# Two attention and mixture-of-experts blocks on one core: expert results scattered to token order by GpSimd inside the expert phases, in place of gathers behind them

## What is computed

```python
x = x + xattn0(layernorm(x), ctx)          # 16 heads of 16
x = x + ffn0(layernorm(x))                 # layer 0
x = x + xattn1(layernorm(x), ctx, mask)
x = x + ffn1(layernorm(x))                 # layer 1
# ffn: shared MLP + routed experts, E = 16 experts of 256 -> 128 -> 256
#   layer 0: the 4 best experts of a token (from the 2 best of 4 groups), sigmoid weights, times 2.5
#   layer 1: the 2 best experts of a token, softmax weights
#   y[token] = sum over its k experts of w * (silu(x Wg) * (x Wu)) Wd
```

## Time and profile before

| what | value |
|---|---|
| median of 3 runs | 2484.33 us (2482.01 to 2484.53) |
| the profiled execution: its own time | 2487.88 us |
| its span, first to last instruction | 2486.0 us |
| busy share PE / DVE / ACT / POOL | 82% / 59% / 43% / 45% |
| moved by DMA | 292.77 MB, mean 118 GB/s |

### The profile page before, as it was taken

One profiled execution on the slowest core, in us unless ns is written; L12 is line 12 of the kernel. 1 busy time (PEld: TensorE's weight loads), 2 busy tenths in 40 slices (PEclk: granted clock), 3 DMA queues, 4 the chain that ended last, 5 costly groups with the idle time before them and its releaser, 6 DMA issues.

```text
span 2486.0 us, 52846 instructions
## 1 busy us (share of the span) xinstructions
PE 2044.5 (82%) x16352; PEld 1599.3 (64%) x16353; DVE 1467.8 (59%) x4591; ACT 1068.5 (43%) x2276; POOL 1121.9 (45%) x1595
## 2 busy tenths in 40 slices
PE   4999999999965999999948989889998849997000
PEld 3777777777754878777736766666666637786000
DVE  3677777777762444444436877777777624443333
ACT  2555555555522333333325555555555513332000
POOL 1455555555556000000056777777777341001676
PEclk8999999999987999999969999999999969999555
DMA  5222222222226444444434333333333154444555
GB/s 204 58 79 80 79 80 80 82 82 78 76 83 148 150 146 150 151 146 151 149 123 171 102 101 101 103 101 107 98 102 101 41 105 150 150 149 132 177 175 169
DMA packets 206442, 292.77 MB, mean 118 GB/s; under 512 B 34230, under 2 KB 155320, under 8 KB 205880
## 3 DMA queue, kind: packets, MB, share of 16 engines
q1 hardware_dynamic: 164199, 185.12, 22.9%
q0 software_dynamic: 37584, 102.81, 13.2%
q10 hardware_dynamic: 4608, 4.20, 1.3%
HBM read 155.69 MB, written 136.33 MB: 117 GB/s over the span
## 4 chain that ended last, share of the span: by engine, by line
PE 59%; POOL 18%; issue 12%; DVE 4%; DMA 4%; ACT 2%; SPq 1%; POOLq 1%; DVEq 0%; ACTq 0%
PE ps L1435 16%; POOL ygath L615 10%; PE ps L1443 7%; PE ps L1371 5%; POOL xsort L559 4%; PE ps L1448 4%; PE ps L1309 3%; PE ps L1287 3%; PE ps L1321 3%; PE ps L1263 3%; PE ps L1346 2%; PE ps L1380 2%; PE ps L1454 2%; POOL rstd L631 2%; PE ps L1230 2%
## 5 line engine op out<-in xcount | busy, mean ns | idle before, releaser
L1435 PE MATMUL ps<-wgu,ygath 128*128 x1664 | 441.3, 388 | 27.6 <-issue 23.0
L559 POOL DMA_INDIRECT xsort<-xn,xidx x384 | 386.7, 1007 | 134.7 <-issue 133.4
L615 POOL DMA_INDIRECT ygath<-ysort,yidx x384 | 372.5, 970 | 152.1 <-issue 99.1
L928 DVE TENSOR_REDUCE mx<-ps 128x16 f32<-128x1920 f32 x128 | 276.2, 2158 | 191.1 <-PE ps L1287 190.8
L1175 DVE TENSOR_TENSOR ygath<-ygath,ps 128x128 f32<-128x128 f32 x416 | 119.7, 288 | 442.8 <-ACT ygath L842 442.8
L1435 PEld LDWEIGHTS ps<-wgu,ygath 128*128 128x128 f32 x1664 | 285.3, 191 | 73.8 <-issue 51.6
L607 POOL CAST yidx<-rows_of 128x8 uint32 (+1 forms) x64 | 12.9, 201 | 682.2 <-SPq L297 680.4
L1371 PE MATMUL ps<-W,wsgu 128*128 128x256 f32 x1024 | 253.3, 391 | 13.7 <-ACT rt L789 12.9
L846 ACT ACTIVATE ygath<-ps 128x256 f32<-128x256 f32 x416 | 159.8, 384 | 231.4 <-PE ps L1448 231.2
L1443 PE MATMUL ps<-wd,ygath 128*128 x832 | 248.1, 380 | 2.8 <-DVE ygath L1187 2.8
L842 ACT ACTIVATE ygath<-ps 128x128 f32<-128x128 f32 x416 | 115.5, 278 | 301.4 <-PE ps L1435 301.3
(11 more groups left out here) (174 smaller groups left out, 3836.2 us busy)
## 6 DMA issues: line engine op xcount, KB each, us to landing
ygath<-xsort SPq DMA_DIRECT2D x416, 128.0 KB, 2.1
ysort<-ygath SPq DMA_DIRECT2D x208, 256.0 KB, 2.3
based<-XO SPq DMA_DIRECT2D x64, 256.0 KB, 2.3
XB<-in_x SPq DMA_DIRECT2D x32, 256.0 KB
wgu<-in_wgu SPq DMA_DIRECT2D x2, 4096.0 KB, 13.7
XB<-based SPq DMA_DIRECT2D x32, 256.0 KB
X<-based SPq DMA_DIRECT2D x32, 256.0 KB
out_x<-X SPq DMA_DIRECT2D x32, 256.0 KB, 2.3
```

The lines of the kernel that those rows point to most:

```text
L559: e.indirect_dma_start(out=xsort, in_=xn2[s][:, t, :], in_offset=None, out_offset=bass.IndirectOffsetOnAxis(ap=xidx[s][:, t * 4 + k:t * 4 ...
L615: e.indirect_dma_start(out=ygath[s][:, t * 4 + k, :], out_offset=None, in_=ysort, in_offset=bass.IndirectOffsetOnAxis(ap=yidx[s][:, t * 4 ...
L928: e.tensor_reduce(mx[:, r].rearrange("p j t h -> p j (t h)"), ps[:, 4 * s:4 * s + 4, 0:4 * LK].rearrange("p j (x k) -> p j x k", k=LK), AX ...
L1435: mm = e.matmul(ps[:, 2 + h, 0:2 * F], xtT[h][:, c, :], wgu[:, bass.ds(x * (DC * 2 * F) + c * 2 * F, 2 * F)], start=(c == 0), stop=(c == D ...
```

## The change

- A row of `xsort` gets 16 more floats (`ROW` = 272): for each expert, the place (token times k, plus which k) at which the result is to stand in token order. DVE writes them in a new step, `aim_rows`, behind `weigh_experts`: a product of 128 x 128 floats (64 in layer 1) and a sum. The zero rows that fill up a region carry places behind the last token.
- In the expert stage DVE takes the column of the tile's expert out of the loaded rows into `yidx` (one 128 x 1 copy a tile, between `yt` and `hT`), for which it reads four expert numbers into registers each fourth tile. POOL writes each result tile to `yrows` with one indirect DMA. SP's stores are gone, and SP waits for the index copy (`eI`) before it loads over a tile. DVE waits for the scatter (`yst`) of the tile four before when it writes `yt`, where it waited for a store.
- `all_rows`, `find_rows` and all gathers are gone. In attention 1 SP loads the 8 rows of a token with one plain DMA (1 MB a sequence); `pack_weights1` now comes behind POOL's scatters.
- The last pass is unrolled with four buffer sets: SP issues both loads (256 and 512 KB a sequence), DVE adds, ACT issues the store.
- Attention 1's order on POOL, ACT and DVE is changed (`ORDER`); its PE string is the same cycle, begun at another step.
- The write of spare rows at the start is two DMAs, issued once the constants have come.

```diff
-    "Pool1": "rstd1:a xb:b gather:m rstd2:c scatter:d",
+    "Pool1": "xb:a rstd2:b scatter:c rstd1:m",
...
-        xsort = nc.dram_tensor("xsort", [XROWS, D], F32).ap()
-        ysort = nc.dram_tensor("ysort", [NT[0] * P, D], F32).ap()
+        xsort = nc.dram_tensor("xsort", [XROWS, ROW], F32).ap()
+        yrows = nc.dram_tensor("yrows", [YROWS, D], F32).ap()
...
+        def routed(L):
+
+            return yrows[0:NTOK * TOPK[L], :].rearrange("(b t p k) d -> b p t (k d)", b=B, t=QT, k=TOPK[L])
...
                 if L == 1:
+                    e.dma_start(ygath[s][:].rearrange("p (t k) d -> p t (k d)", t=QT),
+                                routed(0)[bass.ds(b, 1)].rearrange("o p t x -> (o p) t x")).then_inc(sig["ld", s], 16)
...
                     for r in range(4):
 
+                        e.wait_ge(eI[r % 2], c2[2 + r // 2])
                         e.wait_ge(eT_ps[r % 2], c2[2 + r // 2])
                         apart(e)
                         load(r, row[r])
-                        if r % 2 == 1 and regs:
-                            store(n - 5 + r, r // 2, c2[r // 2])
...
+            for b in range(B):
+                r = b % 4
+                if b >= 4:
+                    e.wait_ge(fin_st[r], 16 * (b // 4))
+                e.dma_start(Xf[r][:], based[b]).then_inc(fin_ld[r], 16)
+                e.dma_start(Yf[r].rearrange("p (t k) d -> p t (k d)", t=QT), routed(1)[b]).then_inc(fin_ld[r], 16)
...
+            def expert_phase(L):
+
+                t0 = NT[0] // 4 * L
+
+                def step(n, r, w, c2):
+                    if isinstance(n, int) and n < 4:
+                        return
+                    q, h, c = tile(4, r, w, c2)
+                    e.wait_ge(eY[h], c)
+                    apart(e)
+                    i = q + 4 * (1 - r // 4)
+                    e.indirect_dma_start(
+                        out=yrows, in_=yt[q], in_offset=None,
+                        out_offset=bass.IndirectOffsetOnAxis(ap=yidx[:, i:i + 1], axis=0),
+                    ).then_inc(yst[q], 16)
...
-                all_rows()
+                expert_phase(L)
                 if L == 0:
                     pack_weights1()
...
+            for b in range(B):
+                e.wait_ge(fin, b + 1)
+                e.dma_start(out[b], Xf[b % 4][:]).then_inc(fin_st[b % 4], 16)
...
+            def aim_rows(L, u, s):
...
+                apart(e)
+                link(e.tensor_tensor(at_e, oh, bc(dest, 3, E), ALU.mult), "c_rt", s, L, u)
+                e.tensor_reduce(xn2[s][:, :, D:ROW], at_e.rearrange("p t k e -> p t e k"), AX.X, ALU.add)
...
-                        if q % 2 == 0 and not (edge and n < 8 and L == 0):
-                            e.wait_ge(yst[q // 2], (w - 1) * 16)
+                        if not (edge and n < 8 and L == 0):
+                            e.wait_ge(yst[q], (w - 1) * 16)
                         e.tensor_copy(yt[q], ps[:, 6 + h, 0:D]).then_inc(eY[h], 1)
+                    if not (edge and n >= NT[L]):
+                        if r % 4 == 0:
+                            e.load(expert_regs, exp_tab[0:1, bass.ds(n * 2 + 12, 4)])
+                            experts[0] = [e.snap(x, min_val=0, max_val=E - 1) for x in expert_regs]
+                        e.wait_ge(xl[r % 4], 16 * w + 16)
+                        apart(e)
+                        e.tensor_copy(yidx[:, r:r + 1], xt[r % 4][:, bass.ds(experts[0][r % 4] + D, 1)]
+                                      ).then_inc(eI[r % 2], 1)
                     if not (edge and (n < 3 or n > NT[L] + 2)):
                         _, h, c = tile(3, r, w, c2)
                         e.wait_ge(eHT_ps[h], c)
                         e.tensor_copy(hT[h], ps[:, 4 + h, 0:P]).then_inc(eHT[h], 1)
```

More of the change, by code:

```diff
@@ L213, in build @@
         xn = [sb(f"xn{s}", [P, QT, D]) for s in range(2)]
-        xn2 = [sb(f"xn2{s}", [P, QT, D]) for s in range(2)]
+        xn2 = [sb(f"xn2{s}", [P, QT, ROW]) for s in range(2)]
         xnT = [sb(f"xnT{s}", [P, DC, LQ]) for s in range(2)]
@@ L232, in build @@
         ygath = [sb(f"ygath{s}", [P, QT * 4, D]) for s in range(2)]
[L233 to L235 removed]
+        yidx = sb("yidx", [P, 8], U32)
         xidx = [sb(f"xidx{s}", [P, QT * 4], U32) for s in range(2)]
@@ L275, in build @@
         xl = [sem(f"xl{r}") for r in range(4)]
-        yst = [sem(f"yst{r}") for r in range(2)]
+        yst = [sem(f"yst{r}") for r in range(4)]
+        eI = [sem(f"eI{r}") for r in range(2)]
         eT_ps, eT, eGU, eG, eH, eHT_ps, eHT, eD, eY = (
@@ L341, in run_steps, with four @@
             t0, last = NT[0] // 4 * L, NT[L] // 4
-            def four(w, regs, steps, ahead=False):
+            def four(w, regs, steps, par=0, ahead=False):
                 n4 = (w - t0) * 4
@@ L503, in expert_phase @@
                     four(e.snap(w), True)
[L504 to L507, removed]
             e.wait_ge(zero_ok, 1)
-            e.dma_start(xsort[E * REG:XROWS, :].rearrange("(n p) d -> p n d", p=P), bc(zero[:], 1, E)
-                        ).then_inc(zfill, 16)
+            spare = xsort[E * REG:XROWS, :].rearrange("(n p) d -> p n d", p=P)
+            e.dma_start(spare[:, :, 0:ROW - 1], bc(zero[:, 0:ROW - 1], 1, E)).then_inc(zfill, 16)
+            with nc.allow_non_contiguous_dma(reason="one number a spare row, once"):
+                e.dma_start(spare[:, :, ROW - 1:ROW], cc(C_DUMP + E, E).unsqueeze(2)).then_inc(zfill, 16)
             e.wait_ge(init, 6)
@@ L527, in _ @@
             end_phase(e, 4)
[L529 to L539, removed]
-                                ).then_inc(sig["st", s], 16)
-            for s in range(2):
-                e.wait_ge(sig["st", s], ended("st", s) + NIT * 16)
+            for b in range(B):
[4 more added lines that the diff above has]
+                e.dma_start(Yf[r].rearrange("p (t k) d -> p t (k d)", t=QT), routed(1)[b]).then_inc(fin_ld[r], 16)
         @block.gpsimd
         def _(e):
-            e.memset(zero[:], 0.0).then_inc(zero_ok, 1)
+            e.memset(zero[:], 0.0)
             for s in range(2):
@@ L671, in attention_phase @@
                     e.wait_ge(sig["sc", s], at("sc", L, NIT - 1))
+            def expert_phase(L):
[11 more added lines that the diff above has]
+                    ).then_inc(yst[q], 16)
+                run_steps(e, L, step, 2)
+                for q in range(4):
+                    e.wait_ge(yst[q], 16 * (t0 + NT[L] // 4))
             for L in range(2):
@@ L682, in _ @@
                 end_phase(e, 2 * L + 2)
-            for s in range(2):
-                find_rows(s, 0, NIT)
-                gather(1, s, range(QT))
-            with e.Fori(1, NIT) as u:
-                for s in range(2):
-                    e.wait_ge(fin[s], u)
-                    find_rows(s, u, NIT + u)
-                    gather(1, s, range(QT))
         @block.scalar
@@ L856, in _ @@
                 end_phase(e, 2 * L + 2)
+            for b in range(B):
+                e.wait_ge(fin, b + 1)
+                e.dma_start(out[b], Xf[b % 4][:]).then_inc(fin_st[b % 4], 16)
+            for r in range(4):
+                e.wait_ge(fin_st[r], 16 * (B // 4))
         @block.vector
```

162 lines of the change are left out of this document (69 added, 93 removed), and 2 rows, old and new, of the table PER.

## The result

The changed kernel takes **2448.55 us** (median of 4 runs, 2444.13 to 2449.02) against 2484.4 us before (4 runs beside it, 2482.01 to 2484.53). The ratio is 0.9854, its 95% interval 0.9837 to 0.9871. It is faster, by 36 us in place of the 83 forecast, and 2448.55 lies inside the range, near its upper end. The profiled execution has a span of 2447.0 us, 39.0 less than the 2486.0 of before.

What follows compares the result with a forecast made beforehand. Bounds: POOL's gathers in attention 1 and the last pass, a PE-DVE ring without slack in the expert stages, PE in attention 0. Sum -90 - 46 - 5 + 2 + 3 + 53 + 0.5 = -83, so 2401 us; range 2345 to 2452.

Steps and rivals of the forecast that it cites:

- the register load's term: Expert stages, each fourth tile: DVE's register load between `yt` and the index copy adds 0.35 us, bounds 0.05 and 0.6.
- +53: Both expert stages: four index copies and two register loads, 1.02 us a round of 8 tiles, 52 rounds; +16 to +94.
- The ring without slack: Expert stages: PE and DVE wait on each other, 3.26 us for two tiles; anything between `yt` and `hT` lengthens it.
- 19.97 us a half: Attention 1: without gathers PE and DVE set this pace in place of 21.79, for -46 us (-60 to -33).
- little at the end: Attention 1: an unspecified small gain added to 24 halves times 1.82 us, making -46.
- the 345 taken: Last pass: transfer rate in GB/s, 97 us for 33.5 MB; 105 us in place of 195, so -90.
- Landing and packing: Stage ends: scatters landing after both expert stages cost +3 us, POOL packing weights behind its scatters +2.
- The wait that was to go for -5: Start of attention 1: ACT's normalising waits for POOL's 8 gathers of the second sequence; without them -5 us.
- Scatters as the pace of the expert stages: Rival, expert stages: at 2.3 us a scatter +229 in place of +53, 2577 us; chance 0.07 including similar-sized causes.
- Hidden index work: Rival, expert stages: DVE's sequencer runs ahead and one column costs nothing; +5 in place of +53, 2353 us; chance 0.17.
- DVE as the bound of attention 1: Rival, attention 1: 21 us a half in place of 19.97 loses 25 us of the gain, 2426 us; chance 0.13.
- A buffer's cycle as the bound of the last pass: Rival, last pass: buffer cycle, not rate, sets it, 14 us for 4 sequences, 120 us, 2416; no separate chance.

## Why the prediction was wrong in its size

The sign came out, and in each stage what was said to bind it. What failed is the size of the terms, and every stage came out longer than forecast. The sum missed by 44 us of span: 25 in the expert stages, 9 in attention 1, 3 to 4 in the last pass, 5 at the stage ends, 1 or 2 in attention 0. The largest miss is the register load's term: 0.35 us put on a loading tile, 0.69 measured. That 2448.55 lies inside the range is owed to wide bounds: that of the expert stages reached +94.

- **The expert stages, +78 for +53: the step that failed is the register load's.** The forecast had 0.5 us for the load, 0.2 for the register work on both sides, less 0.34 hidden behind `yt`: 0.35, twice in eight tiles. The load itself was about right, 0.60 in one loading tile and 0.34 in the other (0.47 on average), and the 0.34 was hidden. The register work was not 0.2 but some 0.55: the rows of 0.09, 0.19 and 0.06 and the pauses between them (1.17 us from `yt` at 900.06 to the index copy, less 0.60). About half of what stands behind the load belongs to the index copy, its wait for the row and its address, which the forecast counted into the 0.08 of that copy. So the delays were 0.83 and 0.54, 1.37 in eight tiles in place of 0.70, and their mean of 0.69 is over the term's own upper bound of 0.6. The index copy was 0.06, costed at 0.08. 4 * 0.06 + 1.37 = 1.6 us for eight tiles, 1.53 measured, times 52 = +80. The ring without slack is borne out by the load at the head of the step and by experts 1 without a load: nine tenths of the loss go when the load goes from there. The Trainium skill, "DMA: Bandwidth & Descriptors", Latency and other measured facts, has 600 ns as a floor for such a load; DVE's median here is 352 ns and its least 341, so the row decides; some 600 appear in fewer than half of the loads, mostly in each second one.
- **Attention 1, -37.5 for -46.** The forecast's 19.97 us a half was right for the plain loads: with the orders of before a half takes 616.75 / 31 = 19.90, and the stage gains 44.3. The diff also changed the orders, and I costed that at nothing; the half became 20.11 (623.5 / 31), which takes 6.7 back. That is this stage's failed step. The "little at the end" in the -46, 2.3 us, had no row either: the last three halves before the change already took 19.8 each. `aim_rows` is covered, as forecast.
- **The last pass, -86.5 for -90.** 321 to 324 GB/s at a share of 0.95 to 0.97 in place of the 345 taken. The bound was the right one, and so was the cycle of some 10 us: 10.2 with two sets, 10.9 with three. The step that was mis-sized is the rate.
- **Stage ends, +4.9 for 0.** Landing and packing were costed (+1.5 each, +2) and are there: the packing 1.8, the last scatter's landing 2.5 from its start. POOL's drain behind its scatters was not: 4.3 us behind experts 0, 2.8 behind experts 1. Before, POOL's drains of these stages began at 807.6 and 2060.4 us, long before the ends. So SP's first load of attention 1 comes 10.3 us behind the last `yt`, 2.9 before: 7.4 more for the 3.5 costed. The wait that was to go for -5 went: from SP's first load to ACT's first normalised rows it is 14.6 us in place of 23.3. From there to the first `rsum` it is 3.1 longer, and why stays open.
- **Attention 0, +1.7 for +0.5.** In the kernels with the change the stretch from the first `rsum` to the first `hm` is 725.7 to 732.4 us, before 724.7 in the one profile there is. A small loss is likely; what makes it stays open.
- **The rivals.** Scatters as the pace of the expert stages: POOL waits 338 us for `yt`, DVE never for a scatter. The Trainium skill's rule ("SBUF — State Buffer", Who interferes with whom), by which copies of DVE in its fast modes block GpSimd, no run here shows: the 416 scatters took 0.95 to 1.02 us each beside DVE's copies out of PSUM. Hidden index work became true only when it was put where it hides. DVE as the bound of attention 1: at 17.2 of 20 us beside PE's 19.15 it was not. A buffer's cycle as the bound of the last pass: true with two and three sets; with four the cycle is long, 12.8 us, at a DMA share of 0.95 to 0.97.

## What to carry to other kernels

In a ring without slack, ask for every new instruction which idle time it can lie in, and put register work, which the profile's page doesn't count as busy, ahead of a wait and not behind one: the same load moved from behind `yt` to ahead of the wait for silu gave back 66 us. A change that comes with a new order should be costed as two changes, since the order here took back a seventh of what the plain loads gave. Where transfers take the place of a compute engine as the bound, count how many buffer sets it takes until the DMA share is near 1, here four for 0.95; with two, this change was a loss of 1%.

## What the hardware showed beside that

- Four numbers into DVE's registers take 0.34 to 0.36 us in 57 of 104 cases and 0.54 to 0.62 in 45, mostly in turns of one loading tile and the next; why, no run here shows. With the register work around it the whole is 0.9 to 1.2 us from `yt` to the index copy, and DVE stands idle for 0.46 to 0.74 of them.
- POOL's drain takes 4.3 us behind the landing of the last indirect DMAs in experts 0 and 2.8 in experts 1, and the barrier of all engines waits for it. At the ends of the attention stages it takes 2.7 and 1.4. What sets its length, no run here shows.
- More transfers in flight lengthen each: the cycle of a buffer of the last pass is 10.2 us with two sets, 10.9 with three and 12.8 with four, while the rate rises from 199 to 279 and 324 GB/s.
